# Attention latents summed once and stacked as rounded parts, in a two-layer adaLN transformer kernel

## The reference, cut to what matters

```python
q = (x @ Wq + bq).reshape(B, T, H, D)
kv_latent = jax.nn.gelu(x @ Wkd + bkd, approximate=False)   # 64 columns
lat = kv_latent[..., :L] + kv_latent[..., L:]               # L = 32
kv = lat @ Wku + bku
k = kv[..., :C].reshape(B, T, H, D)
v = kv[..., C:].reshape(B, T, H, D)
attn = softmax(where(causal, q @ k.T / sqrt(D), -inf))
out = (attn @ v) @ Wo + bo
```

## Time and profile before

| what | value |
|---|---|
| median of three runs | 646.83 us (646.17 to 647.59) |
| the profiled execution's own time | 646.88 us |
| its span, first to last instruction | 645.0 us |
| mean granted TensorE clock | 0.967 |
| PE busy | 599.1 us (93%) |
| DVE busy | 542.1 us (84%) |
| ACT busy | 487.6 us (76%) |
| POOL busy | 167.7 us (26%) |

### The profile page before, as it was taken

The page is one execution under the profiler, slowest core; times in us unless marked ns, Lnnn a source line. Parts: engine busy times, 40 slices in busy tenths (PEclk is TensorE's granted clock), DMA queues, the critical chain, the costliest instruction groups (busy, mean ns, idle before and its releaser), DMA issues.

```text
span 645.0 us, 10999 instructions
## 1 busy us (share of the span) xinstructions
PE 599.1 (93%) x3297; PEld 441.4 (68%) x3297; DVE 542.1 (84%) x1338; ACT 487.6 (76%) x858; POOL 167.7 (26%) x144
## 2 busy tenths in 40 slices
PE   8799889888999999999999999785898999999996
PEld 5466556555545688888888888354675888888884
DVE  4868888888858868988988888869799789999997
ACT  5658999999647899999999999798635556666663
POOL 4422323223304033553455342040432000000000
PEclk9899999999998999999999999996897999999998
DMA  7000000000100042112201210000000222222201
GB/s 252 1 1 3 1 3 1 1 0 1 34 1 0 6 164 99 52 47 99 98 29 68 98 49 1 1 1 1 0 1 2 69 91 89 91 90 90 91 0 67
DMA packets 6491, 28.83 MB, mean 45 GB/s; under 512 B 862, under 2 KB 990, under 8 KB 4383
## 3 DMA queue, kind: packets, MB, share of 16 engines
q1 hardware_dynamic: 6448, 28.32, 12.4%
HBM read 27.13 MB, written 1.19 MB: 44 GB/s over the span
## 4 chain that ended last, share of the span: by engine, by line
PE 63%; DVE 24%; ACT 6%; issue 4%; DMA 1%; POOL 0%; SPq 0%; DVEq 0%; ACTq 0%; POOLq 0%
PE PS L1213 17%; PE PS L1215 16%; PE PS L1214 16%; DVE STAT L874 9%; PE PS L1364 2%; PE PS L1292 2%; DVE RA L894 2%; PE PS L1319 2%; PE PS L1239 2%; DVE SU L900 1%; DVE HN L680 1%; PE PS L1333 1%; ACT STAT L397 1%; DVE HL L692 1%; ACT RA L635 1%
## 5 line engine op out<-in xcount | busy, mean ns | idle before, releaser
L1015 DVE TENSOR_TENSOR RA<-AR,RA 128x512 fp32r<-128x512 f32 x144 | 137.4, 978 | 26.2 <-ACT RA L518 24.6
L517 ACT ACTIVATE AR<-PS,BI 128x512 f32<-128x512 f32 x144 | 99.8, 693 | 15.3 <-PE PS L1215 7.8
L1213 PE MATMUL PS<-HH,WH 128*128 128x512 f32 x272 | 108.9, 400 | 0.2
L1215 PE MATMUL PS<-HL,WH 128*128 128x512 f32 x272 | 107.1, 394 | 0.0
L1214 PE MATMUL PS<-HH,WL 128*128 128x512 f32 x272 | 107.1, 394 | 0.0
L518 ACT ACTIVATE RA<-PS,BI 128x512 fp32r<-128x512 f32 x144 | 98.7, 685 | 0.0
L874 DVE CUSTOM_DVE_ANT_0 STAT<-PS,MQ 128x128 f32<-128x128 f32 (+1 forms) x256 | 76.3, 355 | 20.0 <-PE PS L1320 19.9
L1213 PE MATMUL PS<-RA,WH 128*128 128x512 f32 x208 | 83.0, 399 | 3.7 <-DVE RA L1179 2.1
L1215 PE MATMUL PS<-RA,WH 128*128 128x512 f32 x208 | 81.2, 391 | 0.0
L1214 PE MATMUL PS<-RA,WL 128*128 128x512 f32 x208 | 81.2, 391 | 0.0
L320 POOL TENSOR_TENSOR AR<-AR 128x512 f32<-128x512 f32 x32 | 50.8, 1587 | 113.2 <-DVE AR L827 113.2
(11 more groups left out here) (212 smaller groups left out, 1164.3 us busy)
## 6 DMA issues: line engine op xcount, KB each, us to landing
AR<-comb SPq DMA_DIRECT2D x15, 1024.0 KB, 4.7
WS<-in_w SPq DMA_DIRECT2D x9, 512.0 KB, 5.5
WS<-in_w SPq DMA_DIRECT2D x7, 384.0 KB, 3.1
M<-in_mats SPq DMA_DIRECT2D x1, 1384.0 KB, 10.8
X<-in_xT SPq DMA_DIRECT2D x4, 256.0 KB, 4.4
out_xT<-X SPq DMA_DIRECT2D x4, 256.0 KB, 2.1
AR<-in_wmod SPq DMA_DIRECT2D x1, 768.0 KB, 7.8
AR<-in_w SPq DMA_DIRECT2D x1, 384.0 KB, 3.1
```

The costliest lines, as they stand in the source:

```text
L517: act.activation(G[:, c, :], PS[:, c, :], ACT.Gelu_apprx_tanh, bias=bias).then_inc(s["act"], 1)
L1015: dve.tensor_tensor(out=GL[:, m0 % 2, c, :], in0=G[:, c, :], in1=f(GH[:, m0 % 2, c, :]), op=ALU.subtract).then_inc(s["lo"], 1)
L1213: pe.matmul(out, wh, xh, start=first, stop=False)
L1215: return pe.matmul(out, wh, xl, start=False, stop=last)
```

## The change

The latent is summed and split before it is used. A new f32 matmul per block, `three_rows(t)` on PE (L1318 in the new file), multiplies GELU's 65 rows (now called LG) by a 0/1 matrix and gives 98 rows in PSUM: the summed latent three times, and two rows of ones. Two DVE instructions per block (`latents(t)`, L875 and L877) turn these rows into rounded and rest parts in LAT (fp32r, 98 rows). The key, value and query-bias weights are split likewise at the start into KMS (fp32r, 98 rows): key and value columns by two DVE instructions (L844, L846), the bias columns by three on POOL (L293 to L296) behind two more sign flips (L289, L290). The projection of keys and the values then have fp32r operands, and a third matmul adds the queries' bias into PSUM. ACT's copies lose the bias, and the two rounding copies become one over both halves. KM grows to 98 x 1250 f32. LL's subtraction moves from the start to POOL's place ahead of the first expert accumulation.

```diff
-        KM = sb("KM", [65, 640])
-        LAT = AR[0:65, 8192:10240]
+        LG = AR[0:65, 8192:10240]
+        KM = AR[0:98, 2048:3298]
+        LAT = RA[0:98, 3072:5120]
+        KMS = RA[0:98, 5120:6272]
+        KMR = RA[0:98, 6272:7424]
+        LATR = RA[0:98, 7424:7936]
@@ POOL
+            gp.tensor_scalar(qb[:, :, 0, :], qb[:, :, 0, :], -1.0, 0.0, ALU.mult, ALU.add).then_inc(qk_bias, 1)
+            gp.tensor_scalar(qb[:, :, 2:4, :], qb[:, :, 2:4, :], -1.0, 0.0, ALU.mult, ALU.add).then_inc(qk_bias, 1)
+            gp.wait_ge(in_vec, 16)
+            gp.wait_ge(qk_bias, 2)
+            gp.tensor_scalar(KMR[:, 640:1152], KM[:, 640:1152], vec("w_sign")[0:98, :], 0.0, ALU.mult, ALU.add).then_inc(qk_bias, 1)
+            gp.tensor_scalar(KM[:, 640:1152], KM[:, 640:1152], vec("w_keep")[0:98, :], 0.0, ALU.mult, ALU.add).then_inc(qk_bias, 1)
+            gp.wait_ge(qk_bias, 4)
+            gp.tensor_tensor(out=KMS[:, 640:1152], in0=KM[:, 640:1152], in1=f(KMR[:, 640:1152]), op=ALU.subtract)\
+              .then_inc(qk_bias, 1)
...
-            gp.wait_ge(l1_split, 1)
-            gp.wait_ge(hn_done, 8)
-            gp.tensor_tensor(out=LL[:, :], in0=lm, in1=f(LH[:, :]), op=ALU.subtract).then_inc(l1_split, 1)
...
             split_hidden(1, HN, 3)
+            gp.wait_ge(l1_split, 1)
+            gp.tensor_tensor(out=LL[:, :], in0=lm, in1=f(LH[:, :]), op=ALU.subtract).then_inc(l1_split, 1)
             experts(0, E0, 1024)
@@ ACT, evac_proj
-                act.activation(QKT[:, 0, :], PS[:, 6, 0:256], ACT.Identity,
-                               bias=KEPT[:, g:g + 1], scale=vec("q_keep")).then_inc(qk_evac, 1)
-                act.activation(QKR[:, 0, :], PS[:, 6, 0:256], ACT.Identity,
-                               bias=SIGNED[:, g:g + 1]).then_inc(qk_evac, 1)
+                act.activation(QKT[:, 0, :], PS[:, 6, 0:256], ACT.Copy, scale=vec("q_keep")).then_inc(qk_evac, 1)
                 act.activation(QKT[:, 1, :], PS[:, 6, 256:512], ACT.Copy, scale=vec("k_keep")).then_inc(qk_evac, 1)
-                act.activation(QKR[:, 1, :], PS[:, 6, 256:512], ACT.Copy).then_inc(qk_evac, 1)
+                act.activation(QKR[:, :, :], PS[:, 6, :].rearrange("p (k n) -> p k n", k=2), ACT.Copy).then_inc(qk_evac, 2)
@@ DVE, before the modulation is evacuated
+            dve.wait_ge(flipped, 2)
+            dve.tensor_scalar(KMR[:, 0:640], KM[:, 0:640], vec("w_sign")[0:98, :], None, ALU.mult).then_inc(kms_done, 1)
+            dve.wait_ge(kms_done, 1)
+            dve.scalar_tensor_tensor(out=KMS[:, 0:640], in0=KM[:, 0:640], scalar=vec("w_keep")[0:98, :], in1=f(KMR[:, 0:640]),
+                                     op0=ALU.mult, op1=ALU.subtract).then_inc(kms_done, 1)
@@ DVE, after the four blocks are normalised
+            def latents(t):
+                dve.wait_ge(sel_psum, t + 1)
+                if t >= 1:
+                    dve.wait_ge(l_done, t)
+                dve.tensor_scalar(LATR, PS[0:98, t, :], vec("lat_sign")[0:98, :], None, ALU.mult).then_inc(lr_done, 1)
+                dve.wait_ge(lr_done, t + 1)
+                dve.scalar_tensor_tensor(out=blk(LAT, t), in0=PS[0:98, t, :], scalar=vec("lat_keep")[0:98, :],
+                                         in1=f(LATR), op0=ALU.mult, op1=ALU.subtract).then_inc(l_done, 1)
+            for t in range(NBLK):
+                latents(t)
@@ PE
+            def three_rows(t):
...
+                pe.wait_ge(lat_done, t + 1)
+                pe.matmul(PS[0:98, t, :], KM[0:65, 1152:1250], blk(LG, t), start=True, stop=True).then_inc(sel_psum, 1)
...
-                pe.matmul(PS[:, 6, 0:256], mat("wq", g), HN[:, cols], start=True, stop=True)
-                pe.matmul(PS[:, 6, 256:512], KM[:, 128 * g:128 * g + 128], LAT[:, cols], start=True, stop=True)\
+                pe.matmul(PS[:, 6, 0:256], mat("wq", g), HN[:, cols], start=True, stop=False)
+                pe.matmul(PS[:, 6, 0:256], KMS[:, 640 + 128 * g:768 + 128 * g], LAT[:, cols], start=False, stop=True)
+                pe.matmul(PS[:, 6, 256:512], KMS[:, 128 * g:128 * g + 128], LAT[:, cols], start=True, stop=True)\
                   .then_inc(proj_done, 1)
...
             project(0, 0, 0)
-            pe.wait_ge(lat_done, 4)
+            three_rows(3)
             for i in range(16):
+                if i % 4 == 0:
+                    pe.wait_ge(l_done, min(i // 4 + 3, 4))
                 mm = pe.matmul(PS[:, 2 + i // 4, 128 * (i % 4):128 * (i % 4) + 128],
-                               LAT[:, 128 * i:128 * i + 128], KM[:, 512:640], start=True, stop=True)
+                               LAT[:, 128 * i:128 * i + 128], KMS[:, 512:640], start=True, stop=True)
```

More of the change, by code:

```diff
@@ L12 @@
 MASKED = -1e30
-VECS = dict(bo=1, bq=4, q_sign=1, q_keep=1, k_keep=1, b1=4 * E0, b2=E0, pb=4, gb=3, fb=3,
-            outb=1, alpha=1, norm=1, norm2=1, bkd=1, c=16, prio=8)
+VECS = dict(bo=1, q_keep=1, k_keep=1, b1=4 * E0, b2=E0, pb=4, gb=3, fb=3,
+            outb=1, alpha=1, norm=1, norm2=1, bkd=1, c=16, prio=8,
+            w_sign=1, w_keep=1, lat_sign=1, lat_keep=1)
 MATS = dict(wkd=64, wq=512, wo=512, router=8, wg=8, l1=4 * 128 + 3 * 384)
@@ L420, in _ @@
                 act.wait_ge(kd_done, t + 1)
-                act.activation(LAT[0:64, t * BLK:(t + 1) * BLK], PS[0:64, t, :], ACT.Gelu, bias=vec("bkd")[0:64, :])\
+                act.activation(LG[0:64, t * BLK:(t + 1) * BLK], PS[0:64, t, :], ACT.Gelu, bias=vec("bkd")[0:64, :])\
                    .then_inc(lat_done, 1)
             def evac_proj(n, g):
-                if isinstance(n, int) and n == 0:
-                    act.wait_ge(qk_bias, 2)
                 act.wait_ge(proj_done, n + 1)
@@ L829, in moe_scale @@
                    .then_inc(s["ymul"], 1)
-            dve.memset(LAT[64:65, :], 1.0).then_inc(latent_one, 1)
+            dve.memset(LG[64:65, :], 1.0).then_inc(latent_one, 1)
             dve.wait_ge(in_vec, 16)
@@ L1282, in _, with latent @@
             pe.wait_ge(in_mats, 16)
-            for t in range(NBLK):
+            def latent(t):
                 pe.wait_ge(hn_done, 2 * t + 2)
@@ L1286, in _ @@
                   .then_inc(kd_done, 1)
+            def three_rows(t):
+                if t == 0:
+                    pe.wait_ge(in_k, 16)
+                    pe.wait_ge(latent_one, 1)
+                pe.wait_ge(lat_done, t + 1)
+                pe.matmul(PS[0:98, t, :], KM[0:65, 1152:1250], blk(LG, t), start=True, stop=True).then_inc(sel_psum, 1)
+            for t in range(3):
+                latent(t)
+            three_rows(0)
+            latent(3)
+            three_rows(1)
+            three_rows(2)
             def keep_clock(count, bank=7):
@@ L1667, in layouts @@
     put("bo", a["L0_attn_bo"])
-    put("bq", heads(a["L0_attn_bq"], 3).T)
-    put("q_sign", np.array([1, -1, 1, 1], f4)[row])
     put("q_keep", np.array([0, 1, 0, 0], f4)[row])
@@ L1681, in layouts @@
     put("bkd", a["L0_attn_bkd"])
+    put("w_sign", np.repeat(np.array([-1, -1, 1, -1, 1], f4), [32, 32, 32, 1, 1]))
+    put("w_keep", np.repeat(np.array([0, 0, 1, 0, 1], f4), [32, 32, 32, 1, 1]))
+    put("lat_sign", np.repeat(np.array([-1, 1, -1, -1], f4), [32, 32, 32, 2]))
+    put("lat_keep", np.repeat(np.array([0, 1, 0, 0], f4), [32, 32, 32, 2]))
     put("c", np.concatenate([a["L0_c"], a["L1_c"]]).T)
@@ L1694, in layouts @@
     wk = np.concatenate([heads(a["L0_attn_Wku"][:, :128], 3).reshape(32, 512), a["L0_attn_Wku"][:, 128:]], 1)
+    bias = np.concatenate([bk.reshape(1, 512), np.zeros((1, 128), f4)], 1)
+    pick = np.zeros((98, 98), f4)
+    pick[np.arange(192) % 64, np.arange(192) // 64 * 32 + np.arange(192) % 32] = 1.0
+    pick[64, 96:98] = 1.0
+    qb = np.concatenate([np.zeros((96, 512), f4), np.tile(heads(a["L0_attn_bq"], 3).reshape(1, 512), (2, 1))])
     rows = np.concatenate([a["L0_attn_bku"][128:], a["L0_ffn_router_b"]])
```

15 lines of the change are left out of this document (6 added, 9 removed).

## The result

The changed kernel takes 658.53 us, median of four runs (656.92 to 660.32), against 646.69 (646.17 to 647.59) for the kernel before on the same chip: a ratio of 1.018, 95% interval 1.015 to 1.021. The forecast was 654.1, with a range of 649.2 to 659.0. The direction is right and the time lies in the range, but the loss is 11.8 us where 7.3 were forecast.

What follows compares the result with a forecast made beforehand. DVE and one round trip to PE were taken to set the attention step. Terms 0 (steps), +5.0 (start), -1.3 (to step 1), +3.1 (LL), +0.5 (clock) gave +7.3 on 646.88, so 654.1 for the median; range 649.2 to 659.0.

Steps and rivals of the forecast that it cites:

- the sum's own range: Whole kernel: 651 to 658 us, with the start and LL each up to 2 us off.
- The attention steps, 0: The 32 attention units: PE and ACT savings lie beside DVE, so no gain; ends 0 and 1.9 us gained.
- Rival 3: Attention steps: projection, copies, join and scores set the step, not DVE; 12.8 us gained, total 641.3; chance 8% with a variant.
- Rival 4: Attention steps: PE's lighter work lets the clock fall, 1.3 us each, ten falls giving 667 us; chance 5%.
- The start, +5.0: Up to the first scores: they come at 33.5 instead of 28.58, +5.0 us; ends +2.2 and +7.6.
- the DMA one: Start: KM's 324 KB more delay KM and M by 0.7 us, KM landing at 12.6.
- the two engines will alternate: Start: POOL and DVE take turns, so the first normalised block comes at 20.2, half way between 17.4 and 22.8: 2.3 late.
- latents: Start: DVE's eight dependent instructions over PSUM take 0.77 us each, 6.1 in all, the last out at 32.0.
- First scores to step 1, -1.3: First scores to step 1: cheaper projections and copies give -0.6, half the slow keep-clock stretch -0.7; ends -2.0 and +0.7.
- LL, +3.1 and +0.5 for the clock: MoE entry: LL holds DVE's L692 for 3.7 us, 0.6 won back; PE's idle clock adds 0.5.
- rival 1: MoE entry: LL is hidden, DVE's L692 and routing run on beside it; total 650.5 us, chance 17%.
- Rival 2: Start: it absorbs most; first scores 2.2 us late, 2.0 won back by step 1; total 650.6, chance 12%.

Runs made afterwards that it cites:

- proj_heavy: Changed kernel with two more key projections per unit, their result overwritten (0.24 us more PE work per step): 660.53 us, ratio 1.020.
- after_again: The changed kernel, unchanged, run again for its second profile: 658.92 us, ratio 1.016 to the kernel before.
- after: First profile of the changed kernel, unchanged, which fell on its slowest run: 660.32 us.
- pool_late: Changed kernel with POOL's bias split and LH moved behind the flips of M and a wait for the four normalised blocks: 655.02 us, 1.010.
- fill: Changed kernel with 12 more keep-clock matmuls in PE's pauses, around the first values, projections and scores: 655.1 us, ratio 1.012.
- ll_back: Changed kernel with LL's subtraction back at its old place in the start, behind LH: 653.66 us, ratio 1.009.
- before_ll_late: Kernel before with only LL moved to where the change puts it, behind the last hidden block's split: 651.19 us, ratio 1.005.
- ll_moe: Changed kernel with LL's subtraction behind the fourth expert addition of layer 0's MoE: 654.86 us, ratio 1.010.
- before_all: Kernel before with LH held until four blocks are normalised, LL in layer 0's MoE, six more keep-clock matmuls between first projections and scores: 644.08 us, 0.995.
- after_all: Changed kernel with LL in layer 0's MoE, bias split and LH held until four blocks are normalised, keep-clock matmuls in PE's pauses: 648.64 us, 1.001.

## Why the prediction was right in direction and too small

The mechanisms were right, and three terms of the sum came out too small: the start by 3.1 us, the way to step 1 by 2.4 (with the wrong sign), LL with its clock by 0.5. A fourth difference, in layer 1, was not in the sum. That the time still lies in the range is due to its width, not to the sum's own range, which ended at 658.

**The attention steps, 0: right.** Measured -0.1, the step 4.39, and `proj_heavy` shows that DVE and its one round trip set it. Rival 3, the projection's chain, and with it the only faster outcome, falls. Rival 4 did not come either: the clock stood at 1.00 from 52 to 190 us.

**The start, +5.0: measured +8.1.** The step that failed first is the DMA one. KM was to be there at 12.6; it was there at 13.24 in one profile and 14.10 in the other, so that the key split, forecast rightly at 1.5 us for its two instructions, ended at 16.31 in `after_again`, and the evacuation of the modulation, queued behind it, starts at 16.23 instead of 14.9. The other profiles tell how much of this is the change. In the four of kernels with the small KM, POOL's first flip begins at 11.40 to 12.78, mean 12.1; in the ten with the large one at 12.48 to 15.25, mean 13.7. So the changed KM lands about 1.6 us later and not 0.7, and the rest of the 14.10 is scatter. The start of the changed kernel hangs on it: in seven of the eight profiles that leave POOL's start as the change made it, the first Wkd matmul comes 8.5 us after this flip, in `after` 8.8, whether the token matmuls ran at half pace or not.

Second, "the two engines will alternate". They did for POOL's first instructions, and then they didn't: DVE was held once, for 3.3 us, until the last four of POOL's row were done, so that from the evacuation to the first Wkd matmul it took 6.0 and 6.4 us where 5.4 were forecast. `pool_late` needs 2.7. Together the first Wkd matmul is 2.3 later than forecast. Third, `latents` took 6.9 us and not 6.1: PE's second `three_rows` was not ready, which left a gap of 0.50, and the wait for the values came with it.

The dependent pairs of `latents` start 0.79 apart for 0.75 us of work, near the 0.77 forecast. The Trainium skill (VectorE: DVE Perf Modes, "The DRAIN you can't avoid") has eight DVE copies take the same time with and without semaphores between them. The trace does not agree for these: a dependent instruction starts 0.04 after the end of the one before, while the independent L684 at 22.34 starts 0.09 before the end of the L688 pair (21.70 + 0.73).

**First scores to step 1, -1.3: measured +1.1.** This term had the wrong sign. I took half of the slow keep-clock stretch back; instead the pauses of PE during the latents brought a longer one, until about 48 us, and scores, projections and keep-clock ran at 1.2 GHz. `fill` shows that 2.3 to 3.3 us hang on it. I had priced it as an open upper end of +0.7, from a stretch as long as that of before, and not asked what the new pause would do to the work behind it. The size of this term scatters: the stretch took 10.92 to 12.00 us in eight profiles of changed kernels without added keep-clock matmuls, and 10.89, 10.89 and 11.81 in three of kernels before.

**LL, +3.1 and +0.5 for the clock: measured +4.1.** The mechanism is as forecast, down to the instruction: DVE's L700 over 3 us long and PE idle beside it. `ll_back`, `before_ll_late` and `ll_moe` each take the gap away or put it in alone, so rival 1 is out. DVE won nothing back there.

**Layer 1, not in the sum: -1.5.** PE's clock stood at 0.91 over 440 to 520 us instead of 0.86. I know of no cause in the change. Layer 1 takes 236.5 to 238.9 us over the fourteen profiles, short ones and long ones with either kernel (236.8 in `before_all`, 238.9 in `after_all`), so this difference may be chance.

**Rival 2,** the start absorbing most, fell with the start's +8.1. The errors are 3.1 (start), 2.4 (to step 1), 0.5 (LL) and -1.5 (layer 1), together the 4.5 us between 7.3 and 11.8.

**One reading of before** was off without harm. The first scores at 28.58 waited for POOL's join, as their row says, and not for the values, which were done at 28.05. The forecast was built on the values, which did set them in the changed kernel.

What stays open: whether KM lands later for its bytes, its 98 rows or its new place, as no run changed one of these alone; when DVE gets a turn between POOL instructions; and what makes layer 1 differ.

## What to carry to other kernels

Look at which engine has slack around the place that work is moved to: the same 3.7 us subtraction cost nothing in the start (first scores at 36.68 in `ll_back`, 36.69 without it), 0.7 in the MoE, 4 to 5 at its entry and 5.6 in the attention steps. Where GpSimd and VectorE both work from SBUF, take the whole row of GpSimd instructions that stand one behind the other as the possible length of a hold, and ask which small VectorE instruction it will catch; here it was four of them in a row, though at other joins VectorE came in between. A pause that is put into TensorE's work can cost more than its length: here the work behind it ran at the lower clock, and twelve matmuls with unused results gave back about 3 us. Compare the same event over all profiles at hand before you explain a difference of 1 or 2 us.

## What was not expected of the hardware

- DVE can go without a turn through four POOL instructions that follow each other: operations over 32 and over 512 columns took 3.34 and 3.94 us there, 0.18 and 0.69 in `pool_late`. One POOL instruction of 3.70 us held operations over one and over eight columns for 3.70 and 3.61 us. At another join DVE did get its turn, and POOL was the one held (0.64 for 0.40 us).
- DVE instructions that read a tile from PSUM, and from SBUF one tile or only a column of scalars, are not held here: 0.75 us beside LL, and 0.75 without it.
- Most of the token matmuls at the very start ran at half pace, 0.85 us from start to start instead of 0.43, in ten of the fourteen profiles, two of them of kernels before, with the granted clock shown as 1.00. The timeline after and before, and the window after:

```profile
5.27 6.41 PE L1249 MATMUL PS<-X,OND 128*128 128x512 f32 x8 [0.78 <-DMA X<-in_xT]
```
```profile
5.13 2.84 PE L1226 MATMUL PS<-X,OND 128*128 128x512 f32 x6 [0.64 <-DMA X<-in_xT]
...
8.19 1.12 PE L1226 MATMUL PS<-X,OND 128*128 128x512 f32 x2 [0.22 <-DMA X<-in_xT]
```
```profile
5.00:11.00 6.00, 5.73 (x7) 2.48 (x8) 1.58 (x3) 1.26 (x2) 0.70 (x5) 1.00 1.02 329
```

Eight instructions took 6.41 us in the changed kernel, and 4.18 before (from 5.13 to 9.31), waits for the tokens included. The clock's own records in the traces say what it was: the first record, of the higher level, begins at 8.93 to 10.75 us in the ten and at 4.09 to 4.99 in the four, and the column counts what lies ahead of the first record as 1.00. So these matmuls ran at the lower level, the column does not tell of the first microseconds, and a difference of about 1 us in the start can be chance.
